# Running the units of the mix stages as one stream with three score slots

## The reference

```python
q = split_heads(x @ Wq); k = split_heads(x @ Wk); v = split_heads(x @ Wv)
scores = jnp.einsum('bqd,bkd->bkq', q, k) / jnp.sqrt(jnp.asarray(D, x.dtype))
attn = jax.nn.softmax(scores, axis=-1)
out = jnp.einsum('bkq,bkv->bqv', attn, v)
...
z = _l2_normalize(z @ Wo); z = _l2_normalize(z @ Wff); z = gelu(z)
```

## Time and profile before

| | |
|---|---|
| three runs, median (lowest, highest) | 6541.54 us (6539.5, 6548.22) |
| the profiled execution: its time, its span | 6545.28 us, 6543.5 us |
| mean granted clock of PE | 0.845 |
| busy, share of the span | PE 78%, PEld 50%, DVE 59%, ACT 66%, POOL 38% |
| bytes moved, mean | 248.00 MB, 38 GB/s |

### The profile page before, as it was taken

The page is one execution under the profiler, slowest core; times in us unless marked ns, Lnnn a source line. Parts: engine busy times, 40 slices in busy tenths (PEclk is TensorE's granted clock), DMA queues, the critical chain, the costliest instruction groups (busy, mean ns, idle before and its releaser), DMA issues. The chain is left out here.

```text
span 6543.5 us, 177007 instructions
## 1 busy us (share of the span) xinstructions
PE 5082.6 (78%) x69200; PEld 3250.3 (50%) x69200; DVE 3856.2 (59%) x6192; ACT 4305.5 (66%) x8847; POOL 2494.6 (38%) x963
## 2 busy tenths in 40 slices
PE   1000069999999999977777899999999998687688
PEld 0000046666666666633333566666666666343443
DVE  4555556666666666655555566666666665546844
ACT  4333347777777777749999677777777776456655
POOL 0000045555555555514444555555555654000000
PEclk6555589999999999976666899999999999667866
DMA  1000022222222222200000222222222221000000
GB/s 48 0 0 0 0 66 55 67 58 60 60 61 64 57 63 60 52 12 1 0 0 1 57 65 59 62 59 64 57 64 60 61 60 41 9 0 3 0 2 7
DMA packets 181302, 248.00 MB, mean 38 GB/s; under 512 B 52076, under 2 KB 80232, under 8 KB 180072
## 3 DMA queue, kind: packets, MB, share of 16 engines
q1 hardware_dynamic: 176264, 221.95, 13.7%
q10 hardware_dynamic: 4320, 15.73, 0.8%
HBM read 43.50 MB, written 5.24 MB: 7 GB/s over the span
## 5 line engine op out<-in xcount | busy, mean ns | idle before, releaser
L401 PE MATMUL PS<-arena 128*128 128x512 f32 x2304 | 1171.0, 604 | 25.8 <-ACT arena L763 17.3
L1070 POOL TENSOR_TENSOR arena<-arena 128x1024 f32<-128x1024 f32 x192 | 551.8, 2874 | 932.7 <-DVE arena L969 932.7
L1070 POOL TENSOR_TENSOR lns<-arena 128x1024 f32<-128x1024 f32 x192 | 543.1, 2828 | 653.5 <-DVE arena L969 640.2
L939 DVE TENSOR_REDUCE arena<-PS 128x16 f32<-128x1024 f32 x192 | 235.1, 1225 | 773.3 <-PE PS L428 773.3
L958 DVE TENSOR_REDUCE arena<-arena 128x32 f32<-128x2048 f32 x192 | 438.9, 2286 | 395.5 <-ACT arena L763 395.5
L1440 PE MATMUL PS<-arena 128*128 128x512 f32 x8 | 5.6, 862 | 803.4 <-DVE arena L1374 803.4
L765 ACT ACTIVATE arena<-PS 128x512 f32<-128x512 f32 x384 | 229.9, 599 | 561.6 <-PE PS L401 558.2
L1073 POOL TENSOR_TENSOR lnc<-arena 128x1024 f32<-128x1024 f32 x192 | 546.5, 2846 | 0.0
L455 PEld LDWEIGHTS PS<-arena 64*64 64x64 f32 x24576 | 472.7, 134 | 145.1 <-issue 137.4
L1073 POOL TENSOR_TENSOR arena<-arena 128x1024 f32<-128x1024 f32 x192 | 541.1, 2818 | 0.0
L762 ACT ACTIVATE arena<-PS 128x512 f32<-128x512 f32 x768 | 481.4, 627 | 66.1 <-PE PS L401 42.8
(11 more groups left out here) (263 smaller groups left out, 11468.3 us busy)
## 6 DMA issues: line engine op xcount, KB each, us to landing
arena<-arena SPq DMA_DIRECT2D x2880, 64.0 KB, 2.0
arena<-in_L_ffn_Wqkv ACTq DMA_DIRECT2D x30, 512.0 KB, 4.1
arena<-in_L_ffn_Wo SPq DMA_DIRECT2D x48, 128.0 KB, 2.8
scratch<-arena SPq DMA_DIRECT2D x4, 1024.0 KB, 4.7
arena<-scratch SPq DMA_DIRECT2D x4, 1024.0 KB, 7.8
arena<-in_L_ffn_W SPq DMA_DIRECT2D x12, 341.0 KB, 3.0
arena<-in_L_ffn_Wqkv SPq DMA_DIRECT2D x6, 512.0 KB, 4.8
arena<-in_ffn_scales SPq DMA_DIRECT2D x12, 128.0 KB, 3.2
```

The costliest lines, as they stand in the source:

```text
L401: pe.matmul(PS[:, QKV + bank, :], xs[uu % 2][:, par * P:(par + 1) * P], w, start=True, stop=True).then_inc(qkv_ready, 1)
L1070: pool.tensor_tensor(halves(heads(t2)), halves(heads(raws[par]))[:, :, ::-1, :], sine, ALU.mult)\
```

## The change

The eight items of a stage become one stream of 64 units (`UNITS_MIX`), written out without a hardware loop. What differs:

- Three slots (`RING = 3`) for scores, exponentials and row statistics; bank 6 (`MIX_OUT`) takes the heads, bank 7 (`MIX_PROJ`) all projections. `scores(u)` waits for the exponentials of u-3.
- PE issues scores(u+2) before heads(u) across items as well. The query and key projections of item b+1 stand ahead of unit 2 of item b, the value projections ahead of unit 4. They read XN itself; the copy `hd_x` is gone.
- ACT copies the next item's keys and queries after unit 3's exponentials, the values after unit 5's, and the finished heads of the item before after unit 0's. The copy of the queries applies the scale, so the exponentials take scale 1.0.
- DVE's reduction writes the negated maximum; the operation that scaled it is gone.
- The four masks move from DVE (a product with a per-partition scalar) to POOL (`mix_gpsimd`, a product of two tiles, the second a broadcast column), one item ahead, with two sets of masked keys, queries and values. POOL had nothing to do in a mix stage before.

```diff
-        hd_e = [hd.take(4 * T).rearrange("p (h t q) -> p h t q", h=2, t=2) for _ in range(2)]
...
+        RING = 3
...
+            def scores(u):
+                b, n = divmod(u, PAIRS8)
+                g = run * B + 1 + b
+                if n == 0:
+                    pe.wait_ge(hd_masked, (g + 1) * HEADS_IN_GROUP)
+                    pe.wait_ge(hd_projected, g * 3 + 2)
+                if u >= RING:
+                    pe.wait_ge(hd_exp, first + u - RING + 1)
...
+            def heads(u):
+                b, n = divmod(u, PAIRS8)
+                if n == 0:
+                    pe.wait_ge(hd_copied, run * B + 1 + b)
+                pe.wait_ge(hd_v_ready, first + u + 1)
...
+            project(0)
+            project_values(0)
+            scores(0)
+            scores(1)
+            for u in range(UNITS_MIX):
+                b, n = divmod(u, PAIRS8)
+                if n == 2 and b + 1 < B:
+                    project(b + 1)
+                if n == 4 and b + 1 < B:
+                    project_values(b + 1)
+                if u + 2 < UNITS_MIX:
+                    scores(u + 2)
+                heads(u)
...
-            act.activation(hd_x, XN[:, ds(b * T, T)], ACT.Copy).then_inc(hd_entered, 1)
...
+            def copy_keys(b):
+                g = run * B + 1 + b
                 act.wait_ge(hd_proj, g * 2 + 1)
...
                 act.wait_ge(hd_masked, g * HEADS_IN_GROUP)
...
+                act.activation(hd_k, PS[:, MIX_PROJ, T:2 * T], ACT.Copy).then_inc(hd_projected, 1)
+                act.wait_ge(hd_scores, (g - 1) * PAIRS8)
+                act.activation(mx_q[b % 2], PS[:, MIX_PROJ, 0:T], ACT.Identity, scale=MIX_SCALE).then_inc(hd_projected, 1)
...
+            def exps(u):
+                st = mx_st[u % RING]
+                act.wait_ge(hd_bias, first + u + 1)
+                if u >= RING:
+                    act.wait_ge(hd_out, first + u - RING + 1)
...
+            for u in range(UNITS_MIX):
+                b, n = divmod(u, PAIRS8)
+                exps(u)
+                if n == 0 and b > 0:
+                    copy_out(b - 1)
+                if n == 3 and b + 1 < B:
+                    copy_keys(b + 1)
+                if n == 5 and b + 1 < B:
+                    copy_values(b + 1)
+            copy_out(B - 1)
...
-                dve.tensor_scalar(hd_m[v], source, hd_only[:, v:v + 1], None, ALU.mult).then_inc(hd_masked, 1)
...
-                    dve.tensor_scalar(st[:, 4:8], st[:, 0:4], -MIX_SCALE, None, ALU.mult).then_inc(hd_bias, 1)
...
+            def shift(u):
+                dve.wait_ge(hd_scores, first + u + 1)
+                dve.tensor_reduce(mx_st[u % RING][:, 0:4], PS[:, 2 * (u % RING):2 * (u % RING) + 2, :]
+                                  .rearrange("p h (t q) -> p (h t) q", t=2), AX_X, ALU.max, negate=True).then_inc(hd_bias, 1)
...
+        def mix_gpsimd(pool, run):
+
+            wait_alone(pool, hd_loaded, 16 * 6 * (run + 1))
+            for b in range(B):
+                g = run * B + 1 + b
+                pool.wait_ge(hd_projected, g * 3 + 1)
+                pool.wait_ge(hd_scores, (g - 1) * PAIRS8)
+                for v in range(HEADS_IN_GROUP):
+                    only = hd_only[:, v:v + 1].broadcast_to([P, T])
+                    pool.tensor_tensor(mx_m[b % 2][v], hd_k, only, ALU.mult).then_inc(hd_masked, 1)
```

More of the change, by code:

```diff
@@ L1620, in mix_sync, with score_banks @@
             sp.dma_start(hd_only, d["c_only"]).then_inc(hd_loaded, 16)
[L1623 to L1630, removed]
+        UNITS_MIX = B * PAIRS8
+        MIX_OUT, MIX_PROJ = 6, 7
+        def score_banks(u):
+            return PS[:, 2 * (u % RING):2 * (u % RING) + 2, :].rearrange("p h (t q) -> p h t q", t=2)
         def mix_tensor(pe, run, call, n0):
@@ L1634, in mix_tensor @@
             wait_alone(pe, hd_loaded, 16 * 6 * (run + 1))
[L1635 to L1673, removed]
+            first = (run * B + 1) * PAIRS8
+            def project(b):
+                g = run * B + 1 + b
+                pe.wait_ge(hd_projected, g * 3)
+                x = XN[:, b * T:(b + 1) * T]
+                for k in range(2):
+                    last = pe.matmul(PS[:, MIX_PROJ, k * T:(k + 1) * T], hd_w[k], x, start=True, stop=True)
+                last.then_inc(hd_proj, 1)
@@ new lines, in heads @@
+            def heads(u):
[3 more added lines that the diff above has]
+                pe.wait_ge(hd_v_ready, first + u + 1)
+                for t in range(2):
+                    for s in range(2):
+                        grp, v = head_of(n, s)
+                        at = grp * VGROUP + v * GROUP
+                        last = pe.matmul(PS[grp * GROUP:(grp + 1) * GROUP, MIX_OUT, 0:T], hd_vm[:, t, at:at + GROUP],
+                                         mx_e[u % RING][:, s, t, :], start=(v == 0 and t == 0),
+                                         stop=(v == HEADS_IN_GROUP - 1 and t == 1), skip_group_check=True)
+                last.then_inc(hd_out, 1)
@@ L1790, in mix_vector @@
+            shift(0)
+            for u in range(UNITS_MIX):
+                if u + 1 < UNITS_MIX:
+                    shift(u + 1)
+                values(u)
             for k in range(2):
@@ L2503, in _ @@
                     b0_gpsimd(pool)
+                if part == "mix":
+                    mix_gpsimd(pool, run)
                 meet(pool, K + 1)
```

123 lines of the change are left out of this document (53 added, 70 removed).

## The result

The changed kernel took 6339.16 us (median of 4 runs, 6336.28 to 6340.42), the kernel before 6544.88 us beside it on the same chip (6539.5 to 6550.9). The ratio is 0.9685, 95% interval 0.9668 to 0.9702: 3.1% faster. The forecast was 6344 us, in a range of 6313 to 6440. The profiled execution took 6338.8 us with a span of 6337.0, 206.5 less than the span of 6543.5 before.

A forecast was written before the change was run, and what follows sets the result against it. PE at 1.2 GHz was taken to bound the mix stages. With the clock at 1.0, both stages fall from 518.8 to 322 us, saving 198 of 6545.3: 6347, less 4 for the runs' median, 6344 us; range 6313 to 6440.

The forecast's parts named there:

- The first claim: Mix stages: inside a batch PE at 1.2 GHz binds; after the change the clock is 1.0 from the first in-stream projection.
- The unit of 2.05 us: PE in the stream at clock 1.0: scores and heads of one unit take 2.05 us, between 1.93 and 2.22.
- The projections, 1.6: PE, per batch at clock 1.0: projections in two places with two switches more take 1.6 us.
- The 0.4 us of clash: PE, per batch: ACT's 0.8 us of key and query copies after unit 3 hold PE up by 0.4 us.
- The start, 18.8 us: Each mix stage from project(0) through project(1), at clock 0.5, takes 18.8 us, including 2.9 for masks.
- A stage of 161 us: One mix stage after the change: 18.8 start, 13.9, seven batches 127.2, last heads 1.06; before, 260.9 us.
- 0.73 us: POOL, one mask of 256 columns, from a line through two measured products; four take 2.9 us, upper bound 9.4.
- two waits of 0.73 us in each batch: DVE against POOL on the shared port: by the skill's rule 20 us over 14 batches, by the median nothing; taken as nothing.
- POOL was not late: Rival, 9%: clock held, but four masks take 9.4 us and PE waits 4 us in each of 14 batches, 6400 us.
- The clock did not swing: Rival, 12%: scores still wait on slots, the clock falls and rises repeatedly, half of 124 units at 3.86 us, 6441 us.
- The fourth rival: Mix stages slower: clock stays at 0.5, 33.8 us a batch against 31.8, 6572 us; chance 7%.
- its 68%: Chance given to the forecast case itself: clock held in the mix stages, PE bound, own range 6313 to 6414 us.

## Why the prediction was right

**The mechanism.** The first claim, that before was bound by PE at 1.2 GHz inside a batch, and that an unbroken stream with the projections in it would hold 2.4 GHz, is shown: by the windows of the changed kernel, by the emptied pipeline (ratio 0.9904), by the narrow projections (1.002), and from the other side by the old kernel with its clock held (0.9777). By that last run some 149 of the 206 us are the clock, and some 60 are the order. The expectation that heads(0) wouldn't lift the clock, and project(1) would, came out to the group: 0.53 until 5676, 1.00 after. By the rule of the Trainium skill, as the prediction read it, the rise would have come with the first heads; it didn't. The Trainium skill's "A second HAM failure mode" describes a clock that swings as PE idles between its groups; the emptied pipeline does that (0.86 and 0.64 in turn), the changed kernel doesn't.

One piece of evidence for the held clock was weaker than it looked. The two stretches of the attention stage at 1.00 with gaps on PE have others beside them in the same stage:

```profile
5974.00:5981.00 7.00, 7.00 (x37) 3.96 (x37) 5.50 (x19) 3.95 (x14) 0.00 (x0) 0.50 0.01 4
```

There the clock stands at 0.50 under a PE without a gap, and at 6002 to 6008 again. That stage shows a clock that comes and goes, not one that holds through gaps. The changed kernel's stream did not put it to the test: PE waited 2.3 us in 140.

**The terms.** The unit of 2.05 us, taken between 1.93 and 2.22, measured 2.05 (1.06 for scores, 0.99 for heads); that a value picked between two bounds met it to the hundredth is luck. The projections, 1.6, measured 1.70 (1.06 and 0.64). The 0.4 us of clash between ACT's copies and the slots was nothing: 8 x 2.05 + 1.70 is 18.10, all of a batch. No run shows this term. The 0.77 us that the third slot is worth is not it, since with two slots the waits are there in the last batch as well, which has none of the copies of keys, queries and values. The start, 18.8 us, was 18.04: four masks took 2.32 us for 2.9, and project(0) ran at the higher level, 1.18 for 2.05. A stage of 161 us was 155.8: 0.8 from the start, 2.1 from seven batches of 18.10 for 18.4, and most of the rest from scores(4) and the last heads (1.0 and 1.06), which I counted beside units that already held them. Each stage was to start 0.55 us sooner; PE's wait ahead of it went from 4.34 to 3.96, so it was 0.4. But for the projections and this, the errors have one sign. With them 206 us were saved for 198, and the profiled execution took 6338.8 us for the 6347 worked out for it.

**The masks on POOL.** 0.73 us was the line through two rows; 0.612 is measured. The Trainium skill's rule on a port pair shared by DVE and GpSimd ("SBUF — State Buffer", "The single rule") was taken at nothing. L1799, the DVE product beside them, has min 191, median 193, max 346 ns. In the changed kernel, and then in the kernel with two units' heads together, a product beside a row of four masks:

```profile
5676.86 2.32 POOL L1827 TENSOR_TENSOR arena<-arena 128x256 f32<-128x256 f32 x4 [14.42 <-ACT arena L1720]
...
5678.89 0.35 DVE L1799 TENSOR_TENSOR arena<-arena 128x32 f32<-128x32 f32 x1
...
5719.52 2.32 POOL L1837 TENSOR_TENSOR arena<-arena 128x256 f32<-128x256 f32 x4 [15.45 <-ACT arena L1730]
...
5720.73 0.59 DVE L1809 TENSOR_TENSOR arena<-arena 128x32 f32<-128x32 f32 x1
```

The trace agrees with the rule. The first product ends at 5679.24, where the last of the four masks ends at 5679.2; each of the 14 products of the changed kernel that start beside a running mask ends 47 to 50 ns after that mask. So DVE waits until the POOL instruction ends, and the price is set by when the product comes. In the changed kernel one product a batch comes late in a mask and loses 0.05 us (0.15 in the row above), 0.8 us in all 14, and nobody waits for it: a batch is as long with the masks on DVE. In the other kernel it comes at a mask's start and loses 0.4 us in each of 14 batches, and there PE waits for it (1.09 us at 5721.38, for 0.69 at the next such place). The prediction's two waits of 0.73 us in each batch did not come because of this order in time, which it had not worked out; taking the term at nothing was right in size by luck.

**The rivals.** POOL was not late (its four masks end some 5 us before the scores that need them). The clock did not swing. The fourth rival, a clock that stays at 0.5, was priced at 33.8 us a batch and 6572 us; it did not happen here, but the kernel with only the idle matmuls ahead shows it at 34.04 us a batch, and the one with its projections cut to eight columns at 32.79 a batch and 6560.6 in all. Its condition, "the clock doesn't rise behind one lone projection", was met in three kernels close to this one, in which project(1) came 0.5 or 1.3 us sooner or 1.4 us later than its 16.05 us after project(0); in one of them seven projections in a row lifted nothing. Nor does that distance decide: with the masks on DVE it is 14.71 us in both stages of one execution, and the rise came 92 and 24 us after the fall; with two slots it is 17.45 and 17.34, and project(1) lifted nothing in the first stage and did in the second. I took the rise behind project(1) for a property of the order, and it hangs on something else besides. It came in the changed kernel, whose four runs lie within 4 us, and so the forecast was right there, but its reason at this point was weaker than its 68% says, and some luck was in it.

**What stays open.** Why one projection lifts the clock and the next doesn't, with the same work on both sides of it, no run here tells. That full-width matmuls are needed is shown; how they must stand is not.

**A version that beats both.** The changed kernel with the clock lifted ahead takes 6322.1 us, a ratio of 0.9657 [0.9641, 0.9673] for 0.9685 [0.9668, 0.9702]. The intervals just touch, and 9 us are gained by the stages' rows. More than these speaks for it that its four runs, and the twelve of the three other kernels built on it, spread by 14 us at the most within a kernel, and their traces show the clock at 1.00 throughout the stages but for 6.8 us at the start of each stage in the one with two slots. Of the twelve runs with two slots alone, with masks on DVE alone and with idle matmuls only ahead, eight took 43 to 187 us more than the changed kernel, the other four 9 to 23.

## What to carry to other kernels

Where matmuls use 32 rows or columns of the array, look at the granted clock before anything else: a PE that is busy all the time can stand at half speed for a whole stage, and a few full-width matmuls put into its waits, useful or not, can be worth more than a new order of the work. If the clock rises inside the stream only at some place, test how firmly: run it several times, move the start by half a microsecond and look again. Costs of single edits (a slot, masks on another engine) are to be measured with the clock held, else they measure the clock.

## What the runs showed of the hardware

- Scores and heads in 32-wide tiles, with full-width matmuls of only 8 columns among them, stayed at 0.50 for 260 us in both stages, with PE busy 255.86 us of it in the first. With full projections among them the stream held 1.00 from 5676 to its end, 138 us, in the changed kernel, and stayed at 0.50 for 264 us in the one with idle matmuls only ahead.
- The level was 1.0 or 0.5 in all stages, and the same instruction group took 1.06 or 1.92 us (heads), 1.13 or 2.08 (scores). An exponential took 0.47 us at both levels, so that at 1.0 ACT nearly binds: with 1.81 us for four of them and 1.6 for a batch's copies, an estimate of some 16 us is the least for a batch, whatever PE does.
- Sixteen scores of two units took 1.16 us, eight took 1.13: groups on different rows of the array ran beside each other.
- A mask of 128x256 took 612 ns on POOL as a product of two tiles, and 285 ns (4 in 1.14 us) on DVE as a product with a per-partition scalar.
- A small DVE product of two operands in SBUF, started while a mask ran on POOL, ended 45 to 50 ns after that mask, in all 28 cases of two kernels: 0.19 us became 0.21 to 0.35 in one and 0.59 in the other, by where in the mask it started.
